# Two-layer decoder on one core: the softmax chain reordered, and both halves of the probabilities turned in one transfer

## What is computed

```python
x = _layernorm(x + _L0_attn_ref(x, ...))        # causal, rotary embedding     (self0)
x = _layernorm(x + _L0_xattn_ref(x, ctx, ...))  # rms norm of queries and keys (cross0)
x = _layernorm(x + _L0_ffn_ref(x, ...))         # 4 experts                    (ffn0)
x = _layernorm(x + _L1_attn_ref(x, ...))        # causal                       (self1)
x = _layernorm(x + _L1_xattn_ref(x, ctx, ...))  # 8 key/value heads for 16     (cross1)
x = _layernorm(x + _L1_ffn_ref(x, ...))         # fp8-rounded products         (ffn1)
# each attention, per head: softmax(q k^T / sqrt(128)) v, then the product with Wo
```

## Time and profile before

| | us |
|---|---|
| median of 3 runs | 2929.32 (2920.0 to 3839.74) |
| profiled execution | 2923.55, span 2921.7 |
| TensorE busy | 2509.2, 86% of the span |
| VectorE busy | 1862.7, 64% |
| ScalarE busy | 1572.5, 54% |
| GpSimd busy | 864.7, 30% |
| share of the transfer queue of SyncE in 16 DMA engines | 41.0% |

### The profile page before, as it was taken

How to read it: one execution, slowest core, us unless ns; L and a number is a source line. 1 busy time by engine, 2 the same in 40 slices (tenths; PEclk the granted TensorE clock), 3 DMA queues, 4 the chain that set the end, 5 groups by cost and what they waited for, 6 DMA issues and landing times. The chain is left out here.

```text
span 2921.7 us, 60581 instructions
## 1 busy us (share of the span) xinstructions
PE 2509.2 (86%) x21768; PEld 1612.3 (55%) x21768; DVE 1862.7 (64%) x3317; ACT 1572.5 (54%) x2742; POOL 864.7 (30%) x741
## 2 busy tenths in 40 slices
PE   6888888888888898888978999989999999986454
PEld 4555555455655565566455666655566666643222
DVE  4666663366665666666155666651688888858886
ACT  4666663176766666666043555550577777732321
POOL 4556555400110010012232212223100000146675
PEclk9999998999999999999988999999999999998777
DMA  3333333144444444446230333341477777852000
GB/s 96 71 71 92 68 73 81 47 89 92 97 95 91 95 91 96 93 94 124 80 151 21 85 88 87 88 94 46 84 146 145 143 151 145 153 115 77 20 0 29
DMA packets 752867, 263.39 MB, mean 90 GB/s; under 512 B 724816, under 2 KB 724816, under 8 KB 751184
## 3 DMA queue, kind: packets, MB, share of 16 engines
q1 hardware_dynamic: 750960, 255.48, 41.0%
q0 software_dynamic: 1760, 5.77, 0.7%
HBM read 82.84 MB, written 2.10 MB: 29 GB/s over the span
## 5 line engine op out<-in xcount | busy, mean ns | idle before, releaser
L786 ACT ACTIVATE ph<-p,ri 128x1024 bf16<-128x1024 f32 (+4 forms) x512 | 437.4, 854 | 461.6 <-DVE ri L1056 394.9
L1066 DVE SCALAR_TENSOR_TENSOR pl<-p,ri,ph 128x1024 bf16<-128x1024 f32 (+4 forms) x512 | 517.4, 1010 | 129.6 <-issue 83.5
L1122 PE MATMUL ps<-wo_hi,v_hi 128*128 128x128 bf16 x2688 | 487.2, 222 | 79.4 <-DMA wo_lo<-pl 79.3
L1123 PE MATMUL ps<-wo_lo,v_hi 128*128 128x128 bf16 x2688 | 487.0, 222 | 0.0
L1124 PE MATMUL ps<-wo_hi,v_lo 128*128 128x128 bf16 x2688 | 486.9, 222 | 0.0
L797 ACT ACTIVATE p<-p,nb 128x1024 f32<-128x1024 f32 (+4 forms) x512 | 435.7, 851 | 48.4 <-DVE nb L1049 33.9
L1122 PEld LDWEIGHTS ps<-wo_hi,v_hi 128*128 128x128 bf16 x2688 | 266.7, 99 | 142.9 <-DMA wo_lo<-pl 96.0
L1122 PE MATMUL ps<-k_hi,q_hi 128*128 128x512 bf16 (+3 forms) x768 | 277.2, 361 | 45.9 <-issue 30.1
L1123 PEld LDWEIGHTS ps<-wo_lo,v_hi 128*128 128x128 bf16 x2688 | 266.9, 99 | 39.1 <-issue 0.8
L1124 PE MATMUL ps<-k_hi,q_lo 128*128 128x512 bf16 (+3 forms) x768 | 277.1, 361 | 0.0
L1123 PE MATMUL ps<-k_lo,q_hi 128*128 128x512 bf16 (+3 forms) x768 | 276.9, 361 | 0.0
(11 more groups left out here) (197 smaller groups left out, 6066.4 us busy)
## 6 DMA issues: line engine op xcount, KB each, us to landing
raw_kv<-in_wkvself SPq DMA_DIRECT2D x32, 512.0 KB, 3.9
raw_q<-in_wqself SPq DMA_DIRECT2D x32, 256.0 KB, 2.7
wo_hi<-ph SPq DMA_TRANSPOSE x512, 3.1
wo_lo<-pl SPq DMA_TRANSPOSE x512, 3.1
raw_q<-in_woself SPq DMA_DIRECT2D x32, 256.0 KB, 2.8
raw_q<-in_wqcross SPq DMA_DIRECT2D x32, 256.0 KB, 2.7
raw_q<-in_wocross SPq DMA_DIRECT2D x32, 256.0 KB, 3.0
raw_kv<-in_wkvcross SPq DMA_DIRECT2D x24, 256.0 KB, 3.1
```

Of the source, the lines that this page charges most:

```text
L786: nc.scalar.activation(m["ph"][:, qt % 2, 0:w], m["p"][:, qt % 2, 0:w], ACT.Copy, scale=ri[:, qt % 2:qt % 2 + 1]).then_inc(p_norm, 1)
L1066: nc.vector.scalar_tensor_tensor(out=m["pl"][:, qt % 2, 0:w], in0=m["p"][:, qt % 2, 0:w], scalar=ri[:, qt % 2:qt % 2 + 1], in1=m["ph"][:, ...
L1122: nc.tensor.matmul(o, l(0), r(0), start=first, stop=False)
L1123: nc.tensor.matmul(o, l(0), r(1), start=False, stop=False)
```

## The change

The chain is closed within one step as far as it goes. ScalarE now runs `rounded` for this step's tile right after its exponential, ahead of the jobs; VectorE runs `inverse` for this step's tile after `remainder` of the tile before, also ahead of the jobs. `heads_out` goes behind the jobs on both engines. `ph` and `pl` become one tile `phl` with the high half in columns 0 to w and the low half in w to 2w, and one crossbar transfer turns both after `remainder`; `tr_in[qt]` then counts 16 in place of 32. `pT[qt]` holds first the high, then the low blocks. Of the two `unit` functions in the diff the first is ScalarE's, the second VectorE's.

```diff
-            m["pT"] = [t[:, 0:QT * L.kt * P].rearrange("p (i k q) -> p i k q", i=QT, k=L.kt) for t in tail]
+            pairs = [t[:, 0:QT * L.kt * P].rearrange("p (i k q) -> p i k q", i=2, k=2 * L.kt) for t in tail]
+            m["pT"] = [pairs[i // 2][:, i % 2, :, :] for i in range(QT)]
...
-            m["ph"] = sb(f"ph{li}", [P, 2, L.kv], BF16, s)
-            m["pl"] = sb(f"pl{li}", [P, 2, L.kv], BF16, s)
+            m["phl"] = sb(f"phl{li}", [P, 2, 2 * L.kv], BF16, s)
...
                     sp.wait_ge(p_norm, at(count, n, it))
-                    sp.nop(nofuse=True)
-                    sp.dma_start_transpose(m["pT"][0][:, qt, 0:w // P, :], m["ph"][:, qt % 2, 0:w]).then_inc(tr_in[qt], 16)
                     sp.wait_ge(p_lo, at(count, n, it))
                     sp.nop(nofuse=True)
-                    sp.dma_start_transpose(m["pT"][1][:, qt, 0:w // P, :], m["pl"][:, qt % 2, 0:w]).then_inc(tr_in[qt], 16)
+                    sp.dma_start_transpose(m["pT"][qt][:, 0:2 * w // P, :], m["phl"][:, qt % 2, 0:2 * w]).then_inc(tr_in[qt], 16)
...
                 def unit(n, it):
                     for qt in range(QT):
-                        if n or qt:
-                            rounded(*((n, it, qt - 1) if qt else (n - 1, it, QT - 1)))
                         act.wait_ge(s_max, at(lambda n: CREDIT + c["s"] + QT * n + qt + 1, n, it))
...
                         nc.scalar.activation(prob, prob, ACT.Exp, scale=1.0 if L.rms else -1.0, bias=nb[:, qt % 2:qt % 2 + 1], accum_out=rs[:, qt % 2:qt % 2 + 1]).then_inc(p_exp, 1)
+                        rounded(n, it, qt)
+                        job_parts(n, it, qt, L.jobs(n, qt))
                         if qt == QT - 1 and n:
                             heads_out(n - 1, it)
-                        job_parts(n, it, qt, L.jobs(n, qt))
...
                 def unit(n, it):
                     for qt in range(QT):
                         prior = (n, it, qt - 1) if qt else (n - 1, it, QT - 1)
-                        if n or qt:
-                            inverse(*prior)
                         scores(n, it, qt)
                         if n or qt:
                             remainder(*prior)
+                        inverse(n, it, qt)
+                        job_parts(n, it, qt, L.jobs(n, qt))
                         if qt == QT - 1 and n:
                             heads_out(n - 1, it)
-                        job_parts(n, it, qt, L.jobs(n, qt))
...
-                    pe.wait_ge(tr_in[qt], at(lambda n: 32 * (c["u"] + n + 1), n, it))
+                    pe.wait_ge(tr_in[qt], at(lambda n: 16 * (c["u"] + n + 1), n, it))
...
-                        last = three(ps[:, O_BANK + n % 2, qt * P:qt * P + P], lambda k: m["v"][k][:, v, kt, :], lambda k: m["pT"][k][:, qt, kt, :], kt == 0, kt == blocks - 1)
+                        last = three(ps[:, O_BANK + n % 2, qt * P:qt * P + P], lambda k: m["v"][k][:, v, kt, :], lambda k: m["pT"][qt][:, k * blocks + kt, :], kt == 0, kt == blocks - 1)
```

More of the change, by code:

```diff
@@ L783, in rounded @@
                     if bn >= 0:
-                        act.wait_ge(tr_in[bq], at(lambda n: 32 * (c["u"] + behind(n, qt, 2)[0] + 1), n, it))
+                        act.wait_ge(tr_in[bq], at(lambda n: 16 * (c["u"] + behind(n, qt, 2)[0] + 1), n, it))
                     act.wait_ge(r_inv, at(lambda n: c["s"] + QT * n + qt + 1, n, it))
-                    nc.scalar.activation(m["ph"][:, qt % 2, 0:w], m["p"][:, qt % 2, 0:w], ACT.Copy, scale=ri[:, qt % 2:qt % 2 + 1]).then_inc(p_norm, 1)
+                    nc.scalar.activation(m["phl"][:, qt % 2, 0:w], m["p"][:, qt % 2, 0:w], ACT.Copy, scale=ri[:, qt % 2:qt % 2 + 1]).then_inc(p_norm, 1)
                 def unit(n, it):
                     for qt in range(QT):
-                        if n or qt:
-                            rounded(*((n, it, qt - 1) if qt else (n - 1, it, QT - 1)))
                         act.wait_ge(s_max, at(lambda n: CREDIT + c["s"] + QT * n + qt + 1, n, it))
@@ L816, in _ @@
                 units(act, unit)
-                rounded(UNITS - 1, None, QT - 1)
                 heads_out(UNITS - 1, None)
@@ L1062, in remainder @@
                     if bn >= 0:
-                        dve.wait_ge(tr_in[bq], at(lambda n: 32 * (c["u"] + behind(n, qt, 2)[0] + 1), n, it))
+                        dve.wait_ge(tr_in[bq], at(lambda n: 16 * (c["u"] + behind(n, qt, 2)[0] + 1), n, it))
                     dve.wait_ge(p_norm, at(lambda n: c["s"] + QT * n + qt + 1, n, it))
                     dve.nop(nofuse=True)
-                    nc.vector.scalar_tensor_tensor(out=m["pl"][:, qt % 2, 0:w], in0=m["p"][:, qt % 2, 0:w], scalar=ri[:, qt % 2:qt % 2 + 1],
-                                                   in1=m["ph"][:, qt % 2, 0:w], op0=ALU.mult, op1=ALU.subtract).then_inc(p_lo, 1)
+                    nc.vector.scalar_tensor_tensor(out=m["phl"][:, qt % 2, w:2 * w], in0=m["p"][:, qt % 2, 0:w], scalar=ri[:, qt % 2:qt % 2 + 1],
+                                                   in1=m["phl"][:, qt % 2, 0:w], op0=ALU.mult, op1=ALU.subtract).then_inc(p_lo, 1)
                 def unit(n, it):
@@ L1096, in _ @@
                 units(dve, unit)
-                inverse(UNITS - 1, None, QT - 1)
                 remainder(UNITS - 1, None, QT - 1)
```

## The result

The changed kernel takes 3195.49 us (median, 3194.22 to 3197.86), the kernel before on the same chip 2927.48 us: a ratio of 1.0925, 95% interval 1.0906 to 1.0944. The ratio compares the fast runs alone and so leaves out one run of the kernel before, of 3839.74 us, which the median of 2927.48 includes. The prediction was 3245 us with a range of 3100 to 3360. The profiled execution after took 3197.86 us, with a span of 3196.0; against the span before (2921.7) that is 274.3 us more.

What follows compares the result with a forecast made beforehand. The prediction took TensorE and the almost equally long VectorE-ScalarE chain as bounds, the chain becoming longer. Cross1 149, cross0 59, self0 88 and self1 26 sum to 322 us on 2923.55: 3245 us, range 3100 to 3360.

Steps and rivals of the forecast that it cites:

- The bound: Whole kernel: VectorE's and ScalarE's chain is almost as long as TensorE's work, so lengthening it shows; TensorE's share near 77%.
- Bare `rounded`, cross1: Cross1: `rounded` loses its cover, `hi` starts 1.5 us later; a pair of units takes 37.9 us against 31.4.
- The new wait, cross1: Cross1: `rounded` waits about 1.5 us for the transfer in two of eight steps; with the bare pass, +149 us.
- Cross0: Cross0: K steps lengthen to 6.03 us, the last shortens to 7.6 by earlier QN; +59 us over 32 units.
- the stalls at each turn of the loop: Cross0: TensorE's stalls of 3.75 us at each turn of the loop sit where TensorE is the bound, and stay.
- Self1: Self1: the chain, with transfer wait and turns, takes 12.8 us per unit against 12.0; +26 us.
- Self0: Self0: `rounded` ahead of the jobs adds 2.8 us per unit with no gap to absorb it; +88 us.
- Rival 1: Self stages and cross0: one issue per tile removes TensorE's waits, QN gives 34 us; faster, 2818 us; chance 4%.
- Rival 2: All stages: TensorE stays the bound, long steps average with empty ones; within 2%, about 2930 us; chance 3%.
- Rival 3: All four stages: the serial chain is real but half is absorbed; 3080 to 3140 us; chance 12%.
- Rival 4: Cross1: the merged transfer lands as late as two in a row, stage +283 us; total 3379 us; chance 6%.
- Rival 5: TensorE's clock falls with more idle time; in cross0's last step +70 us, total 3315 us; chance 8%.

Runs made afterwards that it cites:

- Experiment 4: Changed kernel with `rounded` moved behind the jobs, `heads_out` and `rotated` on ScalarE: 2859.95 us, ratio 0.9783 to the kernel before.
- experiment 6: Changed kernel with `rounded` behind the jobs on ScalarE and two transfers per tile in all stages: 2863.84 us, ratio 0.9772 to the kernel before.
- experiment 9: Changed kernel with four buffers of `phl` in place of two in self0, self1 and cross1: 3133.41 us, ratio 1.0727 to the kernel before.
- experiment 8: Changed kernel with GpSimd's weight split in self0 held back until the reciprocal of the unit's last tile: 3172.54 us, ratio 1.0856.
- experiment 1: Changed kernel with `ph` and `pl` as two tiles and two transfers again, new order kept: 3169.08 us, ratio 1.0831 to the kernel before.
- experiment 2: Changed kernel with the old order of `rounded`, `inverse` and `heads_out`, merged transfer kept: 2919.08 us, ratio 0.9988 to the kernel before.
- experiment 5: Changed kernel with `rounded` behind the jobs on ScalarE, merged transfer in self stages only, two in cross stages: 2848.87 us, ratio 0.9724.

## Why the prediction was right

**The bound.** The reading that VectorE's and ScalarE's chain was nearly as long as TensorE's work, and that what is added to it would show, held: the kernel is 9.2% slower with the same work. TensorE's share is 81%, where near 77% was forecast.

**Bare `rounded`, cross1.** Right. K and Q steps are 5.00 to 5.06 us, forecast 5.15; the V step 6.27 to 6.32, forecast 6.45; the empty ones 2.77. `hi` starts 3.78 us into the step and not 3.9, since the reciprocal came at 2.53 and `rounded` took 1.05 to the start of the next instruction and not the 1.15 of its row: rows of one engine overlap by 0.1 us, which counts once for each pass in the chain. Experiment 4 removes the mechanism and the loss with it.

**The new wait, cross1.** Right. Landing forecast 4.3, measured 4.3 us; waits forecast at 1.5 us in two steps of eight, seen at 1.57 and 1.61. A pair of units takes 39.7 us (2 × 19.86), forecast 40.9; the stage +132 us in place of +149, by the 0.1 to 0.3 us by which each of six steps is shorter than forecast. The fit that the Trainium skill gives ("DMA: Bandwidth & Descriptors", Anatomy of one DMA) made it 3.2 us; the measurement decides. Its rule to coalesce holds in kind (4.3 us is less than two times 3.1), and was worth 14 us in self1 in experiment 6, but it cost 26 us on top of this order, and on the old one 3 us were left of it.

**Cross0.** The steps were right: 5.94 to 6.00, 5.93 to 5.99, 5.78 to 5.85 and 7.56 us against 6.03, 6.03, 5.95 and 7.6. The last step's gain from QN was right too: 1.13 us per unit, 36 us, against 1.1 and 34. The step that failed is "the stalls at each turn of the loop [...] stay": they cost 1.39 us per unit before (25.14 on average against 23.75 away from a turn), and 1.0 after (26.22 against 25.22). That a chain longer than TensorE's work hides part of a stall of TensorE fits this, but no run isolates it. Together with 0.38 us per unit on the steps (25.22 against 25.6) that is +35 and not +59 us.

**Self1.** The term was mis-sized, +26 for +6. Away from the turns the unit is 11.8 us (2.64, 3.11, 1.57, 4.45), where 12.15 + 0.5 was forecast. Two sizes failed, each by some 0.45 us: the Q step is 2.64 and not 3.1, even shorter than before (2.88), and the last step is 4.45 with its wait for the transfer, where 4.4 + 0.5 was forecast. With four buffers (experiment 9) the K step and the last one are each 0.14 us shorter, so the wait is worth 0.28 us of such a unit; over the whole stage, turns included, the unit falls by 0.5 us (12.16 to 11.66). The other way, the turns of the loop kept 0.36 us per unit of the 0.8 before, and 0.15 was forecast. Why the Q step is so short stays open.

**Self0.** Mis-sized the other way, +107 for +88. In units without the split the steps are 3.45, 4.83, 3.43 and 4.35, a unit of 16.06 against the 16.6 forecast (their mean is 16.0); in those with it 18.15. The missing term is the contention: it was there before, at 0.45 us in every other unit, and the new order moved `k_lo` (1.01 us in the line shown, 2.3 to 2.4 now) right behind the start of GpSimd's split. Moving the split away gives back 23 us by experiment 8. I had costed what follows the exponential and had not looked at what runs on GpSimd at the new time.

**The total.** Part of its closeness is luck: cross0, self1 and cross1 came 24, 20 and 17 us under their terms and self0 19 us over, by a cause that the sum did not have.

**The rivals.** Rival 1 (the transfers decide) falls with experiments 1 and 2; its part about QN was a true gain, 45 us alone and 36 in this kernel. Rival 2 (TensorE stays the bound) falls with its share of 84% in cross1. Rival 3 was right for self1 and partly for cross0. Rival 4 (two in a row) falls with the landing. Rival 5, the clock: the granted clock fell from 0.95 to 0.89 in self0 and from 0.99 to 0.94 in cross1, 0.945 to 0.929 over the span. In those two stages the steps are accounted for by VectorE's and ScalarE's instructions. The two engines together wait for TensorE only 8.2 us in the whole of cross1 and 11.3 us in self0, so the lower clock did not set the steps. For cross0's last step no run separates it; at 0.98 there is little to find.

**What stays open.** Why self0 gains nothing from the merged transfer (44.8 us of waits in experiment 2 against 43.5, and units of 13.47 and 13.44 us in experiments 5 and 6), though the issues of SyncE are halved there; and what the turns of the loop hide exactly. No run isolates either.

## What to carry to other kernels

A pass is free where its engine is idle anyway, and costs its whole length where the other engine of the chain waits: before moving an operation "earlier", ask what stands beside it at the new place, what queues behind it on its in-order engine, and what a third engine does to the same memory at that time. An early result is worth something only to someone who waits for it: the 0.15 us of QN, moved forward alone, gave 45 us; the 1.15 us of `rounded` moved forward, with the wait and the collision that came along, cost 335. Merging two transfers saves the second's issue, but the whole then leaves with the later half and holds its buffer until the larger landing, so count the slack of the buffer together with the order.

## What the runs showed of the hardware

- **VectorE beside GpSimd.** With all operands in SBUF, `k_lo` took 0.69 us alone and 2.38 beside GpSimd's split, and `remainder` of 384 columns 0.61 and 1.60 us. With one of its inputs in PSUM such an instruction was not slowed: in experiment 8 `v_lo`, of the same size, runs beside one of GpSimd's splits 16 times and takes 690 to 692 ns each time. `q_lo`, with both inputs in SBUF, runs beside GpSimd's rotation and takes 1.21 us in nearly every unit of self0, before as after. The Trainium skill states the rule ("SBUF — State Buffer", SBUF: two separate sides): a VectorE instruction with two inputs in SBUF and a GpSimd instruction that reads SBUF hold one pair of ports exclusively, for a whole instruction. The trace agrees: `k_lo` ended 0.54 us after the split did (344.22 and 343.68), little less than its own 0.69, as if it had started only then.
- **Turning transfers.** Columns to landing, issued from SyncE, out of and into SBUF: 2.4 us at 320 (mean), 3.1 at 1024, 4.3 at 2048. The issue hardly depends on the size: 1.23 and 1.32 us. Merging two of 1024 columns saves an issue, and 4.3 us is less than two times 3.1; the low half alone lands 3.1 us after its issue, the merged one 4.3.
